# Four 64x64 quarters for scores and contexts in every second pair of a two-layer graph attention kernel

## What is computed

```python
for l in range(2):
    h = relu(layernorm(x))                       # x: (128 graphs, 128 nodes, 384)
    q, k, v = heads(h @ Wq + bq), heads(h @ Wk + bk), heads(h @ Wv + bv)
    scores = einsum('bhqd,bhkd->bhqk', q, k) / sqrt(64) + where(adj, 0, -9e15)
    ctx = einsum('bhqk,bhkd->bhqd', softmax(scores), v)
    x = x + ctx @ Wf + bf
```

## Time and profile before

| | us |
|---|---|
| median of 3 runs (lowest, highest) | 1846.69 (1845.74, 1847.37) |
| profiled execution | 1845.01 |
| span of its instructions | 1843.2 |
| busy: PE | 1821.0 |
| busy: DVE | 1624.0 |
| busy: ACT | 1560.5 |
| busy: POOL | 1491.2 |

### The profile page before, as it was taken

One profiled execution on the slowest core, in us unless ns is written; L12 is line 12 of the kernel. 1 busy time (PEld: TensorE's weight loads), 2 busy tenths in 40 slices (PEclk: granted clock), 3 DMA queues, 4 the chain that ended last, 5 costly groups with the idle time before them and its releaser, 6 DMA issues.

```text
span 1843.2 us, 54371 instructions
## 1 busy us (share of the span) xinstructions
PE 1821.0 (99%) x17234; PEld 1050.1 (57%) x17234; DVE 1624.0 (88%) x5551; ACT 1560.5 (85%) x4793; POOL 1491.2 (81%) x1781
## 2 busy tenths in 40 slices
PE   8899999999999999999999999999999999999998
PEld 3455555555555555555555555555555555555555
DVE  7888989898898988889898988989888898989886
ACT  5888888888888888888888888888888888888884
POOL 4678888888888888888888888888888888888762
DMA  6656666666766667666766666666666676666655
GB/s 204 174 171 190 208 198 195 192 209 200 210 195 199 199 194 211 195 204 189 210 201 205 204 198 194 199 203 211 192 197 200 203 211 194 196 191 192 183 170 193
DMA packets 439942, 363.32 MB, mean 197 GB/s; under 512 B 207700, under 2 KB 406888, under 8 KB 439656
## 3 DMA queue, kind: packets, MB, share of 16 engines
q1 hardware_dynamic: 439656, 359.86, 64.8%
HBM read 184.30 MB, written 175.37 MB: 195 GB/s over the span
## 4 chain that ended last, share of the span: by engine, by line
PE 91%; DVE 3%; ACT 1%; issue 1%; POOL 1%; DMA 1%; SPq 1%; DVEq 0%; ACTq 0%; POOLq 0%
PE ps_qk L683 13%; PE ps_shared L683 13%; PE ps_shared L685 13%; PE ps_shared L684 13%; PE ps_qk L685 13%; PE ps_qk L684 13%; PE ps_shared L780 7%; PE ps_scores L803 7%; SPq L375 1%; DVE largest L1181 1%; DMA p_dram<-p_blocks 1%; ACT probs L1020 1%; DVE p_blocks L1264 0%; DVE probs L1323 0%; POOL probs L551 0%
## 5 line engine op out<-in xcount | busy, mean ns | idle before, releaser
L1020 ACT ACTIVATE probs<-probs,row_min 128x128 f32<-128x128 f32 x1512 | 582.9, 390 | 2.5 <-DVE row_rcp L1288 1.5
L551 POOL TENSOR_TENSOR probs<-probs,row_rcp 128x768 f32<-128x768 f32 x252 | 370.2, 1469 | 213.2 <-DVE row_rcp L1288 213.0
L1323 DVE CUSTOM_DVE_ANT_0 probs<-ps_scores,mask,minus_scale 128x128 f32<-128x128 f32 x1512 | 429.6, 348 | 0.9 <-issue 0.6
L568 POOL TENSOR_TENSOR p_half<-p_moved,p_half 128x768 f16<-128x768 f32 x236 | 388.1, 1645 | 0.4 <-ACT p_half L995 0.2
L1303 DVE SCALAR_TENSOR_TENSOR qk_lo<-ps_qk,qk_bias,qk_hi 128x512 f16<-128x512 f32 x384 | 278.6, 748 | 64.0 <-ACT qk_hi L1003 62.9
L1020 ACT ACTIVATION_READ_ACCUMULATOR probs<-probs,row_min 128x1 f32 x1512 | 287.2, 190 | 0.0
L1003 ACT ACTIVATE qk_hi<-ps_qk,qk_bias 128x512 f16<-128x512 f32 x384 | 257.6, 671 | 15.3 <-PE ps_qk L685 15.3
L1334 DVE SCALAR_TENSOR_TENSOR x_tile<-ps_shared,out_scale,x_tile 128x384 f32<-128x384 f32 x256 | 157.6, 616 | 118.2 <-PE ps_shared L685 116.8
L547 POOL TENSOR_TENSOR x_tile<-x_tile,out_bias 128x384 f32<-128x384 f32 x256 | 257.6, 1007 | 1.6 <-DVE out_bias L1247 1.6
L683 PE MATMUL ps_shared<-wf_hi,ct_hi 128*128 128x384 f16 x768 | 250.4, 326 | 0.8 <-DVE ct_lo L1297 0.8
L684 PE MATMUL ps_shared<-wf_lo,ct_hi 128*128 128x384 f16 x768 | 250.4, 326 | 0.0
(11 more groups left out here) (156 smaller groups left out, 3980.4 us busy)
## 6 DMA issues: line engine op xcount, KB each, us to landing
p_dram<-p_blocks SPq DMA_DIRECT2D x256, 384.0 KB, 2.4
p_moved<-p_dram SPq DMA_DIRECT2D x1008, 96.0 KB, 2.3
h_dram<-h_blocks SPq DMA_DIRECT2D x252, 192.0 KB, 2.5
h_moved<-h_dram SPq DMA_DIRECT2D x1008, 48.0 KB, 2.0
x_tile<-in_x SPq DMA_DIRECT2D x128, 192.0 KB, 2.8
out_x<-x_tile SPq DMA_DIRECT2D x128, 192.0 KB, 2.7
adj_u<-in_adj SPq DMA_DIRECT2D x64, 64.0 KB, 2.5
p_half<-p_dram SPq DMA_DIRECT2D x16, 96.0 KB, 2.1
```

The costliest lines, as they stand in the source:

```text
L551: nc.gpsimd.tensor_tensor(probs_of(t, i), probs_of(t, i), row_rcp[i % 2][:, :].rearrange("p (a o) -> p a o", o=1) .to_broadcast([P, HEADS, ...
L568: nc.gpsimd.tensor_tensor(p_part(i, 1), p_moved[i % 2][:, :, :].rearrange("p a n -> p (a n)"), p_part(i, 0), ALU.subtract).then_inc(p_set, 1)
L1020: ins = nc.scalar.activation(tile[:, s, :], tile[:, s, :], ACT.Exp, bias=row_min[i % 2][:, s:s + 1], scale=-1.0, accum_out=row_sum[i % 2][ ...
L1323: ins = nc.vector.tensor_tensor_reduce(tile[:, s, :], score_bank(i, s // PAIRS)[:, (s % PAIRS) * P:(s % PAIRS + 1) * P], mask[b][:, i, :], ...
```

## The change

- `PIECES`: piece 8 moves from position 1 to the head of position 2. So chunk 2 ends at position 2, in its first part.
- At position 1 the last piece (now 7) is issued after the output instead of before the values.
- At position 2, where both context graphs are halved (slots 3 to 61), the scores are issued as 64x64 quarters (each score matmul in two, by halves of the queries), and the contexts as 64x64 quarters (each in two, by halves of the keys). In phase 0 the first graph takes keys 0 to 63 and the second keys 64 to 127, in phase 1 the other way round. The order is score, phase 0, score, phase 1. Phase 1 waits for phase 0 (`ctx_begun`).
- The waits of both contexts stand in `contexts_free`, ahead of the first of these scores.

```diff
-    PIECES = (((0, 1), (2, 3)), ((4, 5), (6, 7, 8)), ((9, 10), (11, 12)), ((13, 14), (15, 16, 17)))
+    PIECES = (((0, 1), (2, 3)), ((4, 5), (6, 7)), ((8, 9, 10), (11, 12)), ((13, 14), (15, 16, 17)))
...
+            def contexts_free(t, i):
+                eu, ei = graph_at(t, i, -1)
+                vu, vi = graph_at(eu, ei, 8)
+                pe.wait_ge(v_set, unit_count(vu, PER, vi + 1))
+                pe.wait_ge(out_added, unit_count(t, PER, i - 1))
+                pe.wait_ge(p_set, halved_count(t, i))
+
+            def half_contexts(graphs, phase):
+                if phase == 1:
+                    pe.wait_ge(ctx_begun, 2 * (graphs[1][0] - HALVED + 1))
+                for c in range(PAIRS):
+                    for k, (a, b) in enumerate(((0, 0), (1, 0), (0, 1))):
+                        for g, (t, i) in enumerate(graphs):
+                            keys = slice(((g + phase) % 2) * DH, ((g + phase) % 2 + 1) * DH)
+                            turned = p_part(i, b).rearrange("p (a s k) -> p s a k", a=QUADS, s=HEADS)
+                            for odd in range(2):
+                                hd = 2 * c + odd
+                                last = c == PAIRS - 1 and k == 2
+                                mm = pe.matmul(ctx_bank(i)[odd * DH:(odd + 1) * DH, c * P:(c + 1) * P],
+                                               v_part(t, i, a)[keys, hd * DH:(hd + 1) * DH],
+                                               turned[keys, odd * PAIRS + c, :, :],
+                                               start=phase == 0 and c == 0 and k == 0, stop=phase == 1 and last)
+                            if last:
+                                mm.then_inc(ctx_summed if phase else ctx_begun, 1)
...
+            def score_quarters(t, i):
+                b = unit_no(t) % 2
+                pe.wait_ge(masked, unit_count(t, PER, i - 1))
...
+                        for odd in range(2):
+                            rows = slice(odd * DH, (odd + 1) * DH)
+                            for half in range(2):
+                                part = slice(half * DH, (half + 1) * DH)
+                                mm = pe.matmul(score_bank(i, odd)[part, c * P:(c + 1) * P],
+                                               q[b][rows, c, i * NODES + half * DH:i * NODES + (half + 1) * DH],
+                                               k[b][rows, KT + c, cols], start=first, stop=last)
+                mm.then_inc(scored, 1)
...
             def slot(t):
                 for i in range(PER):
...
-                    if exists(t) and i % 2 == 0:
-                        score(t, i)
-                        score(t, i + 1)
-                    for pu, pi in pair_at(t, i):
-                        if exists(pu):
+                    pair = [(pu, pi) for pu, pi in pair_at(t, i) if exists(pu)]
+                    if exists(t) and i == 2 and len(pair) == 2 and halved(pair[0][0]) and halved(pair[1][0]):
+                        contexts_free(*pair[1])
+                        score_quarters(t, i)
+                        half_contexts(pair, 0)
+                        score_quarters(t, i + 1)
+                        half_contexts(pair, 1)
+                    else:
+                        if exists(t) and i % 2 == 0:
+                            score(t, i)
+                            score(t, i + 1)
+                        for pu, pi in pair:
                             apply_probs(pu, pi)
+                    pieces = PIECES[i][0] + PIECES[i][1]
+                    late = pieces[-1:] if i == 1 else ()
                     if exists(t + 1):
-                        for piece in PIECES[i][0] + PIECES[i][1]:
+                        for piece in pieces[:len(pieces) - len(late)]:
                             project_qk(t + 1, piece)
                     if exists(t + 1):
                         project_v(t + 1, i)
                     if exists(ou):
                         output(ou, oi)
+                    if exists(t + 1):
+                        for piece in late:
+                            project_qk(t + 1, piece)
```

More of the change, by code:

```diff
@@ L258, in build @@
         ctx_summed = sem("ctx_summed")
+        ctx_begun = sem("ctx_begun")
         ct_hi_set = sem("ct_hi_set")
@@ L805, in score @@
                 mm.then_inc(scored, 1)
+            def score_quarters(t, i):
+                b = unit_no(t) % 2
+                pe.wait_ge(masked, unit_count(t, PER, i - 1))
+                cols = slice(i * NODES, (i + 1) * NODES)
+                for c in range(PAIRS):
+                    for q, k, first, last in ((qk_hi, qk_hi, True, False), (qk_hi, qk_lo, False, False),
+                                              (qk_lo, qk_hi, False, True)):
+                        for odd in range(2):
[6 more added lines that the diff above has]
+                mm.then_inc(scored, 1)
             def output(t, i):
```

## The result

The changed kernel takes 1974.38 us (median of 5 runs, 1973.84 to 1975.68), the kernel before 1846.86 us on the same chip: a ratio of 1.0694, 95% interval 1.0681 to 1.0706. The forecast was 1955 in a range of 1925 to 2000.

What follows compares the result with a forecast made beforehand. PE was taken as the bound, busy 1821.0 of 1843.2 us, so every new wait counts in full. +1.79 us in 59 slots (105.6) plus 3 took the profiled 1845.0 to 1953.6, the median to 1955; range 1925 to 2000.

Steps and rivals of the forecast that it cites:

- Quarters: Scores and contexts at position 2: four quarter matmuls together in 0.056 us, one changeover gained, block 2.23 to 2.11 us, -0.12 a slot.
- contexts_free: Ahead of the first score quarters at position 2: PE waits for DVE's residual until 927.18, a stall of 0.44 us.
- a sign of being wrong: Listed as showing the forecast wrong: no wait at piece 12, fours further apart than 0.06 us, or p_set released last.
- What the late piece hides: Piece 7, issued after the output at position 1, hides 0.65 us of the residual; without it the stall would be 1.09.
- Piece 12: Last piece of position 2: due at 931.90, waits for DVE's qk_lo of chunk 2 until about 933.37, stall 1.47 us.
- The sum: Per slot -0.12 + 0.44 + 1.47 = +1.79 us; 59 slots give 105.6 us, slots 1 and 2 another 3.
- Eight instructions in 0.056 us therefore fit: Step for the quarters on PE: six instructions of one score begin within 0.02 us, so a four takes 0.056 us.
- The count of 1925 to 1980: Times given by the prediction's own case, at 72%, for stalls of 1.3 to 2.2 us in sum.
- Two by two: Rival: quarters on PE don't run four together, +2.0 us on 59 slots, 118 us, so 2073 us; 14%.
- only the residual's wait: Rival: piece 12 is covered after all, leaving the wait ahead of the scores; +19 us, 1866 us; 5%.
- Faster with both waits hidden: Rival: the changeover is gained and neither wait reaches PE; 7 us less, 1840 us; 5%.
- Everything a little longer: Rival: another engine late in turn, POOL's p_lo being only 0.2 us ahead of the residual; 1975 us; 4%.

## Why the prediction was right, and where it was short

**Quarters.** A four at 0.056 us was right (rows 1052.68 and 1052.74 above, and 36 in 0.50 us). Block 2.14 against 2.11: -0.09 a slot instead of -0.12.

**contexts_free.** The residual was forecast to begin at 926.42; it began at 1051.98 - 125.56 = 926.42. PE came 0.09 us after its end, not 0.14, and that is the whole difference. PE was due at 1051.98 + 0.22 + 0.10 of changeover = 1052.30, which is 926.74 with 125.56 taken off and was forecast as 926.73. So 0.38 to 0.39 against 0.44; with the waits behind the first score the slot fell by the same 0.39. `p_set` wasn't last, but near it: POOL ended p_lo at 1052.42, 926.86 as forecast. Only in the last slot with quarters was it last (1.6 us longer), which the prediction had named as a sign of being wrong. What the late piece hides was mis-sized (0.65 for 0.50), which touched only a side remark and not the sum.

**Piece 12.** Forecast: due 931.90, resumes 933.37, 1.47 us. Measured, with 125.56 taken off: 931.86, 933.32, 1.46. The chain contexts, ct_hi, ct_lo, six masks, qk_lo held link by link (ct_hi 929.43 for 929.46; masks 930.89 for 930.93; qk_lo 932.52 for 932.56). The two runs that read chunk 2 earlier confirm the two links that can be taken away, p_hi and the masks.

**The sum.** -0.09 + 0.39 + 1.46 = +1.76, the slot's own difference, against +1.79; 59 slots give 104 us for 105.6. The other 27 of the 130.7 us are these, by the steps between the slots' first scores:

- 14 us: eight stalls of 1.5 to 2.2 us in the contexts, PE's supply of instructions. The sum had no such term. Two more, of 1.4 us at 875.00 and 1839.97, stand in the piece behind the quarters and cost nothing: piece 12 waits that much less, and their slots took 29.81 and 29.80 us.
- 6 us in slots 1 and 2, forecast as 3: the wait at piece 12 is 3.5 us in slot 1, and the low clock follows it.
- 4 us: ACT's late `ct_hi` in each fourth slot, not in the sum.
- 1.6 us: the wait for p_lo in the last slot with quarters, and some 1.5 us of small delays in a few slots and ahead of the first.

The step of the prediction that failed is "Eight instructions in 0.056 us therefore fit", and only in what it left out. That they follow one another so fast was true. But it argued from six instructions of one burst of a single position, and put at nothing the question whether 288 of them in 2.1 us are there to be followed: eight times they weren't, for 14 us. The row of the instruction queue (137 packets) stood on the page before and wasn't read. The count of 1925 to 1980 for stalls of 1.3 to 2.2 us also leaves out the changeover's -0.12; with it it is 1919 to 1972. The measured 1974 lies in the stated range and the two waits are right, but that it came so close to 1980 is the doing of terms that the sum doesn't have.

**The rivals.** "Two by two" is refuted by the x4 rows, "only the residual's wait" by piece 12. "Faster with both waits hidden" could be built: with its two waits removed, the quarters still gave 1856.87 us and not 1840. The gain of 0.10 us a slot was there in 24 slots, and late transfers of the probabilities, which reach PE through the residual and qk_lo, took more than all of it. "Everything a little longer" (1975) hit the number by luck: most of the missing time is PE lacking instructions, and of what it named (another engine late in turn, by p_lo) the record shows 1.6 us in one slot, besides ACT's 4 us.

## What to carry to other kernels

When a step of one engine is moved past a position, look for the buffer that its result shares with a later step, and then for the reader's place in the orders of the *other* engines: here two thirds of the loss was that ACT and DVE read chunk 2 at their usual place, behind p_hi and six masks, and one move on each of them gave back 84 us. A wait hoisted to the head of a block should be put behind whatever in the block doesn't need it (0.39 us a slot), and each wait as far back as its own reader allows, for the time by which it is hoisted is slack against late transfers that is given away. And splitting matmuls to fill the array better multiplies the instructions: count them per microsecond of burst, and read the instruction queue's row beside the busy times. Last, a median slot and a total don't tell why a gain of 0.1 us a slot is missing; the list of single slots does.

## What the runs showed of the hardware

- Four 64x64 quarters, each with its own weights, run side by side: x4 rows 0.056 us apart, 36 such matmuls in 0.50 us, so 14 ns from one matmul to the next. The Trainium skill, "TensorE: Matmul & The Clock Gate", section "Wait — 56ns, not 53.3ns?", has start-to-start never under some 25 ns; the rows of this kernel don't agree with that as a rule for matmuls in different quarters, and the +1.6 us a slot that the prediction worked out from it didn't come.
- A change of the array's shape costs 0.09 to 0.12 us, between 64x128 and 128x64 as between 64x128 and 64x64.
- PE's instructions come in blocks of 16.4 KB, about 250 of them. When a block's edge fell into the burst of 288 instructions in 2.1 us, and PE had stood at a wait just ahead of the burst, PE stood still for 1.5 to 2.2 us, until 2.2 to 2.7 us after a packet of the instruction queue had begun. With the wait behind the first score the longest was 0.6 us. 36 instructions put in once in slot 1 moved the stalls in all later slots, so a small edit anywhere can shift such a loss.
- A wait of 1.5 us of PE in each slot of 29.8 us left the granted clock at 1.00 in the stretch from 300 to 1700 us, the 2.4 GHz level. Behind the wait of 3.5 us at 91.56 it was 0.50, the 1.2 GHz level, until 97.2. In the kernel with the quarters and the old pieces it fell to 0.50 twice for some 3 us (734.5 to 737.7 and 1058.8 to 1062.0), each time behind a wait of 0.8 us and, 2 us after its end, a stall of 1.9 us; in that kernel's other slots with such a stall it stayed at 1.00.
